# An expert layer's second weights: from a load per tile to one resident copy in SBUF

## What is computed

```python
# graph layer, adj: 128 x 128 x 128
n   = layernorm(x)
h   = silu(rmsnorm((adj @ n + eps * n) @ W1 + b1) * rms_w)      # 128 -> 512
x   = x + h @ W2 + b2                                          # 512 -> 128
# experts: E = 16, two for each row, F = 256
u   = layernorm(x)
top = top_k(u @ gate_w + gate_b, 2);  w = softmax(top)
y_e = relu(u @ w1[e] + b1[e]) @ w2[e] + b2[e]                   # 128 -> 256 -> 128
out = x + layernorm(u + sum over both experts of w * y_e) * gamma + beta
```

## Time and profile before

| | us |
|---|---|
| median of 3 runs | 849.93 |
| lowest, highest | 845.57, 850.3 |
| the profiled execution | 851.24 |
| its span | 849.5 |
| mean granted clock of TensorE | 0.947 |

### The profile page before, as it was taken

One profiled execution on the slowest core, in us unless ns is written; L12 is line 12 of the kernel. 1 busy time (PEld: TensorE's weight loads), 2 busy tenths in 40 slices (PEclk: granted clock), 3 DMA queues, 4 the chain that ended last, 5 costly groups with the idle time before them and its releaser, 6 DMA issues.

```text
span 849.5 us, 18665 instructions
## 1 busy us (share of the span) xinstructions
PE 738.6 (87%) x4709; PEld 569.3 (67%) x4710; DVE 626.3 (74%) x2290; ACT 528.6 (62%) x1123; POOL 518.5 (61%) x540
## 2 busy tenths in 40 slices
PE   4899999999999999993299999999999999999700
PEld 4577777778877777773177776777776767766500
DVE  3589999999999999886657666466776776666564
ACT  2599999999999999884223332445444445444441
POOL 3004767777677777777430267677777673767774
PEclk9799999999999999997589999999999999999955
DMA  5435555555555543221676788999999999999832
GB/s 159 133 144 175 173 178 167 176 189 190 184 192 178 176 156 105 71 81 55 181 217 191 208 257 240 259 264 265 271 278 267 270 264 268 268 277 259 235 109 80
DMA packets 141242, 165.83 MB, mean 195 GB/s; under 512 B 18803, under 2 KB 94723, under 8 KB 141190
## 3 DMA queue, kind: packets, MB, share of 16 engines
q1 hardware_dynamic: 122614, 129.87, 50.2%
q0 software_dynamic: 16384, 34.11, 13.9%
q10 hardware_dynamic: 2192, 1.31, 0.6%
HBM read 99.67 MB, written 65.55 MB: 195 GB/s over the span
## 4 chain that ended last, share of the span: by engine, by line
SPq 17%; PE 14%; issue 7%; POOL 7%; DVE 5%; DMA 4%; ACT 1%; POOLq 0%; DVEq 0%; ACTq 0%
SPq L379 6%; PE bank L694 6%; PE bank L679 5%; POOL work L499 5%; SPq L387 4%; SPq L396 4%; DMA tin<-dispatched 3%; SPq L398 3%; POOL rows L499 2%; PE bank L668 1%; PE bank L689 1%; DVE tout L1195 1%; ACT rows L752 1%; SPq L426 1%; DMA dispatched<-rows,slot_i 0%
## 5 line engine op out<-in xcount | busy, mean ns | idle before, releaser
L480 POOL DMA_INDIRECT dispatched<-rows,slot_i x256 | 258.6, 1010 | 168.9 <-issue 159.6
L499 POOL DMA_INDIRECT work<-results,place x184 | 184.0, 1000 | 122.3 <-DVE tout L1195 66.9
L812 ACT ACTIVATE hid<-bank,wts 128x256 f32<-128x256 f32 x286 | 120.1, 471 | 219.2 <-PE bank L679 219.2
L1195 DVE SCALAR_TENSOR_TENSOR tout<-bank,gate,tin 128x128 f32<-128x128 f32 x286 | 87.2, 347 | 124.5 <-PE bank L694 120.6
L694 PE MATMUL bank<-wts,hid 128*128 128x128 f32 x1144 | 165.6, 288 | 0.0
L679 PE MATMUL bank<-tut,wts 128*128 128x256 f32 x572 | 149.7, 385 | 5.1 <-DVE tut L1178 5.1
L694 PEld LDWEIGHTS bank<-wts,hid 128*128 128x128 f32 x1144 | 138.4, 191 | 17.1
L531 PEld LDWEIGHTS bank<-w_sb,work 128*128 128x128 f32 x1024 | 122.8, 193 | 17.7 <-issue 14.6
L531 PE MATMUL bank<-w_sb,work 128*128 128x128 f32 x1024 | 125.8, 276 | 1.5 <-ACT work L791 1.5
L525 PE MATMUL bank<-agg,w_sb 128*128 128x512 f32 x256 | 125.0, 611 | 0.0
L679 PEld LDWEIGHTS bank<-tut,wts 128*128 128x128 f32 x572 | 98.5, 192 | 14.5 <-DVE tut L1178 6.2
(11 more groups left out here) (186 smaller groups left out, 1049.1 us busy)
## 6 DMA issues: line engine op xcount, KB each, us to landing
wts<-in_w_exp SPq DMA_DIRECT2D x143, 257.0 KB
tin<-dispatched SPq DMA_DIRECT2D x143, 132.0 KB, 3.7
results<-tout SPq DMA_DIRECT2D x26, 704.0 KB, 5.5
results<-tout SPq DMA_DIRECT2D x143, 128.0 KB
xs<-in_x SPq DMA_DIRECT2D x32, 256.0 KB, 3.3
adj_sb<-in_adj_t SPq DMA_DIRECT2D x32, 256.0 KB
rms_b<-r_row SPq DMA_DIRECT2D x32, 256.0 KB, 3.5
out<-agg SPq DMA_DIRECT2D x32, 256.0 KB
```

The source lines that it names most:

```text
L480: nc.gpsimd.indirect_dma_start(dispatched, bass.IndirectOffsetOnAxis(slot_i[:, k, n:n + 1], 0), rows[:, k, n // TOPK, n % TOPK, :], None). ...
L499: nc.gpsimd.indirect_dma_start(moe_of(g)[:, n // TOPK, n % TOPK, :], None, results, bass.IndirectOffsetOnAxis(place[:, g, n:n + 1], 0)).th ...
L812: last = nc.scalar.activation(hid[:, n % 2, c, :], hid_ps[n % 2][:, c * TILE:(c + 1) * TILE], ACT.Relu, bias=wts[:, k, F + FC * D + c:F + ...
L1195: last = nc.vector.scalar_tensor_tensor(out=tout[:, k, a, :], in0=exp_ps[n % 2][:, a * D:(a + 1) * D], scalar=gate[:, n % 2, a:a + 1], in1 ...
```

## The change

The second layer's weights of all 16 experts (2 MB) are loaded once into a new SBUF buffer `w2_all`, by two DMAs of ScalarE's queue at steps 2 and 3 of the graph layer. The per-tile load `wts` then holds the first layer and `b1` alone. TensorE reads the second layer at the address that the register `e` gives. To make room, `w1t_sb`, used only in the set-up, lies on `hid`, and `t_m`, used only for the table, on `adj_sb`. TensorE waits for `w2_in` once before its first tile.

```diff
-WROW = F + FC * D + FC
+WROW = F + FC
...
-        w1t_sb = sb("w1t_sb", [P, HC, D])
-        t_m = sb("t_m", [P, 2, 2, NQ])
+        t_m = adj_sb[:].rearrange("p k j n -> p (k j n)")[:, 0:4 * NQ].rearrange("p (a b q) -> p a b q", a=2, b=2)
+        w2_all = sb("w2_all", [P, FC, E * D])
+        w1t_sb = hid[:, 0].rearrange("p c n -> p (c n)").rearrange("p (c d) -> p c d", d=D)
+        w2_in = sem("w2_in")
...
                             last = nc.tensor.matmul(exp_ps[n % 2][:, a * D:(a + 1) * D],
                                                     hid[:, n % 2, c, a * P:(a + 1) * P],
-                                                    wts[:, k, F + c * D:F + (c + 1) * D],
+                                                    w2_all[:, c, bass.ds(e, D)],
                                                     start=False, stop=(a == TH - 1 and c == FC - 1))
...
             pe.wait_ge(b2_in, 16)
+            pe.wait_ge(w2_in, 16 * FC)
             pipeline(pe, tile_step, *P2, RING2)
...
+                if i is None and 2 <= t < 2 + FC:
+                    act.dma_start(w2_all[:, t - 2, :], w2_exp[:, t - 2, :]).then_inc(w2_in, 16)
...
-                            bias=wts[:, k, F + FC * D + c:F + FC * D + c + 1], scale=2.0)
+                            bias=wts[:, k, F + c:F + c + 1], scale=2.0)
...
-                nc.vector.tensor_copy(w1t_sb[:].rearrange("p c d -> p (c d)"), h_ps[0][:, :]).then_inc(gram_ev, 1)
+                nc.vector.tensor_copy(hid[:, 0].rearrange("p c n -> p (c n)"), h_ps[0][:, :]).then_inc(gram_ev, 1)
...
-        a["L0_ffn_w2"].reshape(E, FC, P, D).transpose(0, 2, 1, 3).reshape(E, P, FC * D),
+    w2_exp = a["L0_ffn_w2"].reshape(E, FC, P, D).transpose(2, 1, 0, 3).reshape(P, FC, E * D)
```

More of the change, by code:

```diff
@@ L37, with gnn_moe @@
 NQ = NS * E
-WROW = F + FC * D + FC
+WROW = F + FC
 LN_EPS = 1e-5
 RMS_EPS = 1e-6
-def gnn_moe(nc, x, adj_t, eps, w1, b1, rms_w, w2, b2, gate_w, gate_b, w_exp, b2_exp, gamma, beta, out):
+def gnn_moe(nc, x, adj_t, eps, w1, b1, rms_w, w2, b2, gate_w, gate_b, w_exp, w2_exp, b2_exp, gamma, beta, out):
     fp32, bf16, i32, u32 = mybir.dt.float32, mybir.dt.bfloat16, mybir.dt.int32, mybir.dt.uint32
@@ L1290 @@
         "gate_w": a["L0_ffn_gate_w"], "gate_b": a["L0_ffn_gate_b"],
-        "w_exp": w_exp, "b2_exp": a["L0_ffn_b2"], "gamma": a["L0_ffn_gamma"], "beta": a["L0_ffn_beta"],
+        "w_exp": w_exp, "w2_exp": w2_exp, "b2_exp": a["L0_ffn_b2"], "gamma": a["L0_ffn_gamma"], "beta": a["L0_ffn_beta"],
     }
```

## The result

The changed kernel takes 845.12 us (median of 20 runs, 842.61 to 848.36), the kernel before 850.12 (20 runs): a ratio of 0.9944, 95% interval 0.9928 to 0.9959. It is faster by 5 us, clear of the noise, where I had forecast 12. In six of the nine sets of runs of the experiments TensorE stood idle for up to 25 us at a time and the kernel before took 1262 to 1275 us (the same chip gave 1273.7 us in one set and 849.35 in another), so from those sets I use what single instructions take, and times only where said.

A forecast was written before the change was run, and what follows sets the result against it. SyncE's back-to-back instructions were taken to bound the tiles. 11 + 0.6 - 0.9 = 10.7 us, plus 1 for gathers, gave 11.7: 851.24 - 11.7 = 839.5, or 838 us on the median's scale, range 831 to 852.

The forecast's parts named there:

- What bounds the kernel: Tile stage: SyncE's own back-to-back instructions set the pace, with a floor of 2.38 us per tile step.
- (a) The bytes: Tile loads: halving `wts` from 257 to 129 KB cuts DMA time by bytes, share from 0.94 to 0.84.
- (b) The stretching: SyncE's tile steps: instructions stretched by nearly full DMA engines recover, 11 us gained of a possible 14.
- the first rival: Tile steps: stretching stays, perhaps from SyncE's own burst of four issues; 0 to 4 us gained, 845 to 851, chance 0.24.
- (b) The landing: Tile stage: `tin` loads land in 3.3 us again instead of 3.9, gaining 0.6 us.
- (c) Register addresses: TensorE's second layer: four to eight address operations per tile, hidden behind its issue lead, cost 0.
- the second rival: TensorE's second layer: matmuls at a register address are slow, 0.2 us each, kernel at 930 us; over 858, chance 0.12.
- (d) ScalarE's two issues: Graph layer: two 1 MB loads issued on ScalarE's queue, 0.455 us each, cost 0.9 us in full.
- (e): Set-up buffers: `w1t_sb` on `hid` and `t_m` on `adj_sb` move addresses only, cost 0.
- the gathers: GpSimd's 56 gathers after its last wait for tiles: shorter, gaining 1 us.
- more than forecast: Rival: all 14 us of stretching and pauses go and gathers reach 1.25 us each; 828 to 833 us, chance 0.05.
- The sum: Whole kernel: 10.7 us gained at tile 128, plus 1 us for the gathers, 11.7 us in all.

The follow-up runs named there:

- bias alone: Changed kernel, but after the first six tiles each `wts` load brings only the bias columns, issue kept: 842.39 us, ratio 0.9913 to the kernel before.
- quarter store: Changed kernel, but 22 stores of `out` write one graph of four, issue kept on SyncE: last run 1262.25 us beside 1262.37 for the kernel before.
- missing load issue: Changed kernel without any `wts` load, issue or wait after the first six tiles: ratios 0.9950 to 0.9984 to the kernel before in four sets.

## Why the prediction was off

The runs of 839 to 850 us side by side. "Rest" is the prediction's account: steps between the loads of `tin` in 602 to 793 us, less 2.38 each, less 0.47 per store. "Reads over" sums, from 434 us on, what each table read of the full length takes beyond 0.67 us, worked out from the rows of the reads.

| kernel | us | last wait for tiles ends | rest per step | reads over | DMA share | TensorE waits for `tin` (434 to 785) |
|---|---|---|---|---|---|---|
| before | 850.1 | 766.09 | 0.19 | 12.0 us | 0.94 | 14.1 us |
| changed | 845.1 | 761.20 | 0.12 | 5.5 us | 0.81 | 9.7 us |
| before, stores on ScalarE | 845.2 | 761.01 | 0.17 | 11.9 us | 0.95 | 9.5 us |
| changed, bias alone | 842.4 | 758.64 | 0.09 | 4.1 us | 0.67 | 7.7 us |
| changed, stores on ScalarE | 839.6 | 753.95 | 0.19 | 8.9 us | 0.81 | 6.3 us |

(The rest holds SyncE's waits for unfinished tiles too, 434 to 785 us: 1.3 us before, none in the changed kernel, 2.0 and 4.9 us in the two kernels with stores on ScalarE. The profiled executions enter the tile stage at 431.3, 431.5, 431.6, 429.9 and 428.8 us; in the last two the earlier start is part of the earlier wait. Free of the start is what TensorE needs from the second layer of tile 60 to that of tile 128: 181.7, 176.8, 176.1, 175.3 and 171.7 us, in the order of the rows. From tile 0 to tile 60 it is 152.7 to 154.0 us in all five.)

*What bounds the kernel*: right from the first store of `out` on. SyncE's back-to-back queue set the pace there; taking a store off it about once in four steps moved the time by some 5 us, in both kernels. Before that store no edit changed TensorE's pace, so those tiles were not shown to hang on SyncE. (SyncE's waits were 3.1 us in five, with VectorE's `agg`, not 2.6 in three; nothing hangs on it.)

*(a) The bytes*: right. The share fell to 0.81 (0.84 forecast), and the bias alone brings it to 0.67.

*(b) The stretching*: this is the step that failed, by size. I took 11 us of a possible 14 because "the share falls to where the read was never stretched". The mechanism is there, and it gave 4.9 us. From 602 to 793 us the rest fell from 13.2 us to 8.4, and the 3 us that I had added for the steps from 515 to 602 us did not come: at 584.2 us both kernels stood at tile 60. The inference from a share was the error: the stretch from 480 to 515 us had no store of `out` in it, so it could show nothing of reads behind a store. The 20 reads behind a store held 8.0 of the 12.0 us before and hold 4.3 of 5.5 us after; at a share of 0.67 they hold 3.7 of 4.1. So the load of the DMA engines does count: from 0.94 to 0.81 it halved these reads' stretching and took most of the others'. From 0.81 to 0.67 it took little more, and what stays follows the store's own bytes. The prediction had said of exactly this, in the first rival, that "those rows can't exclude it", and then decided by them. Besides, pauses and longer issues, of which I let 2 us stay, did not shrink: one issue of `wts` takes 0.91 us, where the longest before took 0.46.

*(b) The landing*, 0.6 us: open. The trace of the changed kernel gives no landing time of the `tin` loads. TensorE's waits for `tin` fell from 14.1 to 9.7 us, which is the same gain seen from the other end, and its waits for the transposed tile (DVE's copy) rose from 4.8 to 6.6.

*(c) Register addresses*, 0: right. The matmul takes 275 ns, its 1144 weight loads have 17.2 us of idle time ahead of them in all, before 17.1, and two address operations per tile do for four matmuls (four to eight were expected). This refutes the second rival.

*(d) ScalarE's two issues*, 0.9 us: the charge was too high. The second layer's first matmul starts at 431.5 us, before at 431.3, and TensorE is busy 25.00 of 25 us from 60 to 85. No cost shows; the difference of 0.2 us is small beside the 428.8 to 431.6 us at which the five traces enter that stage.

*(e)* right, and *the gathers*, 1 us: wrong. The 56 gathers take as long as before, with fewer bytes around them. GpSimd's slack held: it still waited 2.48 us at group 25. (In the rival *more than forecast* its 16 us of slack would end the kernel at 834 us, 849.93 - 15.9, and not at 832, had it come to that.)

The sum, with measured sizes: 4.9 us at the last wait, less 0.3 for the gathers behind it, is 4.6 us, the difference of the two profiled spans (849.5 and 844.9).

*The first rival* had the place right, the reads behind the four issues, and its range (845 to 851) held the time. Its cause was not right: the burst of issues doesn't stretch, the store's 256 KB do. What SyncE's fourth issue costs is its own 0.47 us, which both theories had booked as untouchable. Moving it doesn't give all of that back: between the loads of tile 60 and tile 128 lie 17 stores, 8.0 us, and SyncE needs 7.0 us less there in the kernel before and 5.5 us less in the changed one, where its reads at the same time grew from 5.5 to 8.9 us of stretching.

Open: why a read is stretched by a store of another queue at all (a read of memory behind many bytes is the obvious reading, but nothing here separates the path to the memory from the DMA engines); what in time the quarter store and the missing load issue give, since no set with a kernel before of 850 us has them; what sets TensorE's pace up to tile 60; and why issues and pauses didn't shrink when the reads did.

## What to carry over

When an issuing queue is the bound, cost its instructions one by one: a transfer's issue that another engine can take cost 0.47 us here, before any question of bytes, and moving 17 of them gave SyncE back 5.5 to 7.0 of 8.0 us. A stretch that serves as the undisturbed reference must contain the same events as the disturbed one; a mean share of the DMA engines says little about a read that comes right behind a large store. And find the one event at which the end hangs (here GpSimd's last wait for tiles): the times of five kernels follow its place.

## What was unexpected of the hardware

A table read of 0.67 us takes up to 1.06 us with the DMA engines busy only 67%, and 1.39 us where the store was issued 1.1 us earlier by another engine. With a quarter of the store's bytes in the same number of packets it takes 0.69 us. An issue of the same store takes 338 ns on ScalarE (22 of them in the fastest version), 422 on SyncE. A moving operand at a register address cost the matmul nothing: 275 ns (median) at a fixed and at a register address, in 4-byte data.
